# A graph network's first aggregation in 16-bit parts, with first products moved into it and a share of the score subtraction moved to ScalarE

## What is computed

```python
h = relu(layernorm(x))
x = x + gcn(h)      # h @ W0; out[d] = dinv[d] * (sum over edges of dinv[s]*hw[s] + dinv[d]*hw[d]) + b
h = relu(layernorm(x))
x = x + rgat2(elu(rgat1(h)))   # rgat1 with 4 heads, rgat2 with 1
# rgat: xr[r] = h @ W[r] for 3 relations; per edge alpha = leaky_relu(xr[r,dst]@q + xr[r,src]@k)
#       a = softmax of alpha over the edges of one dst;  out[dst] = sum of a * xr[r,src] + b
```

## Time and profile before

| | us |
|---|---|
| median of 3 runs | 1609.46 |
| lowest and highest run | 1606.19, 1611.54 |
| the profiled execution | 1607.11 |
| its span, first to last instruction | 1605.3 |
| PE busy | 1453.7 (91%) |
| DVE, ACT, POOL busy | 901.0, 274.0, 1000.9 |
| mean granted clock of PE | 0.932 of full speed |

### The profile page before, as it was taken

How to read it: one execution, slowest core, us unless ns; L and a number is a source line. 1 busy time by engine, 2 the same in 40 slices (tenths; PEclk the granted TensorE clock), 3 DMA queues, 4 the chain that set the end, 5 groups by cost and what they waited for, 6 DMA issues and landing times.

```text
span 1605.3 us, 24837 instructions
## 1 busy us (share of the span) xinstructions
PE 1453.7 (91%) x6446; PEld 878.0 (55%) x6450; DVE 901.0 (56%) x2002; ACT 274.0 (17%) x709; POOL 1000.9 (62%) x1112
## 2 busy tenths in 40 slices
PE   4988999999978999999699999769996999899996
PEld 2545555555566555666455555455553655455553
DVE  8677722334455888888688878406324445223333
ACT  2545300000011333323000124410110011000000
POOL 1599277666537777882477777336656662777673
PEclk9988999999987999899799999858997999899998
DMA  8300498899831131111588888701231111889898
GB/s 319 118 20 21 125 315 305 291 316 312 270 102 23 51 110 47 40 37 41 169 303 278 285 262 257 241 3 32 59 111 31 40 43 50 286 298 308 281 303 269
DMA packets 86811, 271.80 MB, mean 169 GB/s; under 512 B 32156, under 2 KB 32531, under 8 KB 86743
## 3 DMA queue, kind: packets, MB, share of 16 engines
q0 software_dynamic: 51072, 199.44, 39.3%
q1 hardware_dynamic: 34807, 65.62, 11.4%
q10 hardware_dynamic: 864, 5.90, 1.0%
HBM read 239.28 MB, written 31.62 MB: 169 GB/s over the span
## 4 chain that ended last, share of the span: by engine, by line
PE 61%; DMA 14%; POOL 10%; issue 7%; DVE 5%; ACT 1%; DVEq 1%; SPq 0%; POOLq 0%; ACTq 0%; PEldq 0%
PE ps L1293 12%; PE ps L1320 12%; PE ps L1359 12%; DMA ring<-keys,idxr 8%; POOL ring L519 8%; PE ps L1361 6%; PE ps L1362 6%; PE ps L1190 5%; DMA ring<-rows,idxr 3%; PE ps L1111 1%; PE ps L1236 1%; PE ps L1153 1%; PE ps L1254 1%; DVE zw L1020 1%; DVE hn L1017 1%
## 5 line engine op out<-in xcount | busy, mean ns | idle before, releaser
L1320 PE MATMUL ps<-wreg,hT 128*128 128x384 f32 x1440 | 486.7, 501 | 7.3 <-PEq L1313 6.6
L519 POOL DMA_INDIRECT ring<-keys,idxr x312 | 319.2, 1023 | 189.1 <-DMA ring<-keys,idxr 73.6
L488 POOL DMA_INDIRECT ring<-rows,idxr x304 | 303.7, 999 | 168.8 <-PEq L1348 60.9
L1320 PEld LDWEIGHTS ps<-wreg,hT 128*128 128x128 f32 x1440 | 280.6, 196 | 202.2 <-issue 23.5
L1359 PE MATMUL ps<-ring,zw 128*128 x664 | 224.0, 495 | 15.6 <-DVE zw L1088 15.0
L1293 PE MATMUL ps<-ring,zw 128*128 x664 | 221.3, 495 | 9.6 <-DVE zw L909 9.6
L488 POOL DMA_INDIRECT ring<-rows,idx x152 | 144.7, 952 | 97.1 <-PE ps L1293 66.0
L1359 PEld LDWEIGHTS ps<-ring,zw 128*128 128x128 f32 x664 | 124.7, 191 | 108.7 <-issue 34.2
L1086 DVE TENSOR_TENSOR ring<-ring,al x166 | 159.2, 959 | 39.4 <-SPq L406 30.7
L1293 PEld LDWEIGHTS ps<-ring,zw 128*128 128x128 f32 x664 | 127.5, 193 | 98.1 <-issue 15.3
L1091 DVE TENSOR_SCALAR zw<-iota_f,tl,al 128x128 f32<-128x128 f32 x166 | 60.8, 368 | 154.7 <-PE ps L1362 129.7
(11 more groups left out here) (189 smaller groups left out, 1314.0 us busy)
## 6 DMA issues: line engine op xcount, KB each, us to landing
wreg<-in_L_gnn_W SPq DMA_DIRECT2D x11, 2304.0 KB, 9.8
rows<-stage SPq DMA_DIRECT2D x30, 386.0 KB, 2.8
rows<-stage SPq DMA_DIRECT2D x30, 384.5 KB, 2.9
stT<-targets_row ACTq DMA_DIRECT2D x6, 960.0 KB
ring<-keys,idxr POOLq DMA_INDIRECT x312, 2.5
ring<-rows,idxr POOLq DMA_INDIRECT x304, 4.5
rows<-stT SPq DMA_DIRECT2D x10, 384.0 KB, 2.9
xs<-in_x SPq DMA_DIRECT2D x3, 1152.0 KB, 13.4
```

The source lines that it names most:

```text
L488: nc.gpsimd.indirect_dma_start(ring[:, t % (2 * RING), 0:WIDTH[l]], None, rows[l], bass.IndirectOffsetOnAxis(idx[:, t:t + 1], 0)).then_inc ...
L519: nc.gpsimd.indirect_dma_start(kb[:, n % KSEMS, t % KB, 0:4], None, keys[l], bass.IndirectOffsetOnAxis(idxr[:, t:t + 1], 0)).then_inc(k_in ...
L1320: last = mm(ps[:, 2 * (nt % 2) + h, 0:HALF], hT[:, k, nt * P:(nt + 1) * P], wreg[:, r % 2, k, h * HALF:(h + 1) * HALF], start=(k == 0), st ...
```

## The change

- **16-bit parts.** Each row of h @ W0, times `dinv`, is divided by a power of two of its own (`unit`; `put` is `dinv`/`unit`) and written as two 16-bit parts, upper and lower, side by side in the bytes of the 32-bit row. DVE finds largest and least value of a tile's rows (`peaks`) and makes the scales in three groups of tiles (`SPLITS`: 0 to 6, 7 and 8, 9) in `units`; ACT makes the upper parts, DVE the lower ones (`upper_parts`, `lower_parts`). The parts lie in hT (now laid out by node tile), and rows[0] has the scale as its extra column. The one-hots are 16-bit, scaled by the scale, in a ring of their own. Per edge tile PE runs four 16-bit matmuls (two halves, two parts) where it ran two of 32 bits. A node's own row comes in by four more matmuls that open the accumulator (`open_own`), no longer by DVE.
- **What moves.** The folds of the third relation go behind the pairs of node tiles 0, 1 and 2. The products with relation 0's weights of node tiles 0 to 7 (`EARLY = 8`) go behind `to_features` of the next tile, inside the first aggregation and its tail, with ACT's copy and the write to rows[1] from ACT's queue. They need 1/sqrt(variance) per tile, which DVE makes in `finish0` by an integer start value and four refinements (`inverse_root`, 14 dependent steps). `prepare(R - 1)` and the fill of `stage` go behind the one-hots of node tile 0.
- **Scores.** DVE subtracts for three heads only; ACT adds the fourth head's scores to the negated distance with two passes per pair. Both go to `scored2`, doubled. `MAX_AT` gets its own places for l = 1, `MASKS_AT` starts 16 halves later.

The diff, cut:

```diff
+EARLY = 8
+MASKS_AT = [(SURE_PAIRS - 3) * max(h + 1 - 2 * EARLY, 0) // (LAST_PAIRS_AT - 2 * EARLY) + 2 for h in range(LAST_PAIRS_AT)]
+SPLITS = ((0, 1, 2, 3, 4, 5, 6), (7, 8), (9,))
@@ ACT, behind the products with W0
                 keep_rows(nt, 0)
+                if nt == NT - 2:
+                    for t in SPLITS[0]:
+                        upper_parts(t)
+                if nt == NT - 1:
+                    for t in SPLITS[1]:
+                        upper_parts(t)
             keep_rows(NT - 1, 1)
+            for t in SPLITS[2]:
+                upper_parts(t)
@@ DVE, behind the sort
+            for t in SPLITS[0][5:]:
+                last = peaks(t)
+            units(0, last)
+            for t in SPLITS[0][:-1]:
+                lower_parts(t)
+            for t in SPLITS[1]:
+                last = peaks(t)
+            units(1, last)
+            for t in SPLITS[0][-1:] + SPLITS[1]:
+                lower_parts(t)
+            units(2, peaks(NT - 1))
+            lower_parts(NT - 1)
             prepare(1)
...
+            def begin0(j):
+                V.tensor_scalar(own[:, j % 2, :], ident[:, :], unit[:, j:j + 1], None, ALU.mult).then_inc(own_in, 1)
+                link(V.tensor_tensor(xs[:, j, :], xs[:, j, :], bias[:, :], ALU.add))
...
+            def inverse_root(j):
+                v, y, a = vare[:, j:j + 1], rstd[:, j:j + 1], pw[:, 0, 0:1]
+                link(V.tensor_scalar(v, mv[:, j, 1:2], EPS_LN, None, ALU.add))
+                link(V.tensor_scalar(y.bitcast(I32), v.bitcast(I32), -0.5, float(0x5f375a00), ALU.mult, ALU.add))
+                for n in range(4):
+                    link(V.scalar_tensor_tensor(a, y, v, y, ALU.mult, ALU.mult))
+                    link(V.tensor_scalar(a, a, -0.5, 1.5, ALU.mult, ALU.add))
+                    last = V.tensor_tensor(y, y, a, ALU.mult)
...
             for j in range(NT):
+                begin0(j)
                 with dve.Fori(bnd[j], bnd[j + 1]) as i:
+                    dve.wait_ge(g_in[0], 2 * i + (RING + 3))
                     for b in range(2):
-                        dve.wait_ge(w_used[0], t + (2 * RING - 1))
-                        V.tensor_scalar(zw[:, 0, b, 0, :], iota_f[:, 0:P], targets_at(i, b), row_at(i, b, D, D + 1), ALU.is_equal, ALU.mult).then_inc(w_in[0], 1)
+                        V.tensor_scalar(onehot_at(i, b), iota_h[:, 0:P], targets_at(i, b), row_at(i, b, D, D + 1), ALU.is_equal, ALU.mult).then_inc(w_in[0], 1)
+                if j == 0:
+                    prepare(R - 1)
+                    V.memset(stage[:, :, :], 1.0).then_inc(wq2_done, 1)
@@ PE
+            def early(nt):
+                pe.wait_ge(t_free, NW + NT + nt + 1)
+                for h in range(2):
+                    if nt >= 1:
+                        pe.wait_ge(early_in, 2 * (nt - 1) + h + 1)
+                    for k in range(KT):
+                        last = mm(ps[:, 6 + h, 0:HALF], hT[:, nt, k, :], wreg[:, 0, k, h * HALF:(h + 1) * HALF], start=(k == 0), stop=(k == KT - 1))
+                    last.then_inc(p_ready, 1)
             for j in range(NT + 1):
                 if j < NT:
-                    open_acc(0, j)
+                    open_own(j)
                     with pe.Fori(bnd[j], bnd[j + 1]) as i:
                         for b in range(2):
                             pe.wait_ge(w_in[0], 2 * i + (b + 1))
                             for a in range(2):
-                                last = mm(ps[:, 2 * (j % 2) + a, 0:HALF], zw[:, 0, b, 0, :], row_at(i, b, a * HALF, (a + 1) * HALF), start=False, stop=False, skip_group_check=True)
+                                for part in range(2):
+                                    last = mm(ps[:, 2 * (j % 2) + a, 0:HALF], onehot_at(i, b), parts_at(i, b, a, part), start=False, stop=False, skip_group_check=True)
                             last.then_inc(w_used[0], 1)
+                if j < 3:
+                    last_folds(NF + 2 * j, NF + 2 * j + 2)
                 if j >= 2:
                     for nt in ([j - 2] if j < NT else [j - 2, j - 1]):
                         to_features(1, nt)
+                        if 1 <= nt <= EARLY:
+                            early(nt - 1)
@@ ACT, per pair of edge tiles
+                act.wait_ge(nm_step[l], 2 * i + 2)
+                act.wait_ge(al_step[l], i + 1)
+                for b in range(2):
+                    last = nc.scalar.activation(scored2[:, side, b, 3, :] ..., negm[:, side, b, :] ..., ACT.Identity, bias=score_at(b), scale=-1.0)
+                last.then_inc(far_in, 1)
```

224 lines of the change are left out of this document (147 added, 77 removed).

## The result

| | before | changed |
|---|---|---|
| median of the runs, us | 1608.74 (4 runs) | 1665.2 (4 runs) |
| lowest and highest | 1606.19, 1611.54 | 1663.28, 1670.98 |
| the profiled execution | 1607.11 | 1670.98 |
| its span | 1605.3 | 1667.9 |
| mean granted clock | 0.932 | 0.907 |

The changed kernel is slower: ratio 1.035, 95% interval 1.0326 to 1.0373, or 56.5 us by the medians. The forecast was 1669, in a range of 1612 to 1702.

What follows compares the result with a forecast made beforehand. PE was taken to bind the first aggregation by only 0.04 us per tile over POOL, whose score batches DVE follows in the next stage. Terms 8.2 + 43.3 + 17.4 - 12 + 5 = +61.9 gave 1669 us, range 1612 to 1702.

Steps and rivals of the forecast that it cites:

- Part 1: Splitting rows into 16-bit parts ahead of the gathers: first gather at 207.9 us, +8.2 us (bounds +5 and +12).
- Part 2, the pauses: First aggregation: PE and DVE blocks at node-tile boundaries hold POOL's gathers for 79 us (bounds 66 and 92).
- The slack of 2.2 us: Eight-slot gather ring, 10.0 us against a 7.8 us slot cycle: PE pauses up to 2.2 us cost POOL nothing.
- Last matmul: End of the first aggregation: 501.0 us against 449.5, 7.8 us after the last gather at 493.2.
- The tail: From last aggregation matmul to keys: early products 6 and 7 stretch 10.2 us to 27.6, +17.4 (bounds +14 and +19).
- Part 3: Projections with scores and maxima: DVE lag, shorter DVE passes and quicker POOL gathers give -12 us (bounds 0 and -25).
- Rival C: Projection stage: the whole 64 us of PE come back, the rest as forecast, 1618 us; chance 0.08.
- The clock: PE's granted clock, plus weights and early rows moved beside the gathers: +5 us (bounds 0 and +25).
- rival B: PE's clock falls at each pause, early products 3 to 4 us dearer eight times: +28, 1697 us; chance 0.11.
- Rival D: Aggregation: two 16-bit matmuls cost as much as one of 32 bits, tile stays at 1.29 us: 1684 us; chance 0.04.
- Rival A: Aggregation: ring hides the blocks, each stage takes its busiest engine's need; faster, 1600 or 1570 us; chance 0.15.
- The sum: Whole kernel: 8.2 + 43.3 + 17.4 - 12 + 5 = +61.9 us on 1607.1, giving 1669.0.

Runs made afterwards that it cites:

- the run with six slots: Changed kernel with GpSimd allowed six row tiles in flight instead of eight in the first aggregation: 1689.78 us (one run).
- the run with one head: Changed kernel with VectorE's two passes of each pair cut to one head of four, other maxima left out: 1632.67 us (one run).
- the kernel before with ACT's scores and the other wait: Kernel before plus ScalarE's fourth-head scores, ScalarE waiting for the end of VectorE's first pass instead of an extra signal: 1606.22 us, ratio 0.9963.
- the quarters: Changed kernel with the six early-product blocks between tiles cut into four parts each, placed among the next tile's pairs: 1654.33 us, ratio 1.0287.

## Why the prediction was right, point by point

**Part 1** (+8.2, bounds 5 to 12): +11.2, inside the bounds. The scales of tiles 7 and 8, forecast for 195.6, came at 198.9 in this trace, when ACT, which had waited 3.74 us for them, begins their upper parts. The rest followed at the forecast distance: ACT's last copy ended at 201.0 instead of 197.6, the split at 207.0, and the first gather came 3.9 us behind. The 3 us are no more than what varies between traces of the same code: in the kernel with four early tiles ACT has the same wait (3.75 us), but the scales come at 193.2 and the first gather at 205.5. Over all traces the first gather starts 8.8 us later with the split than without it (209.7 against 200.9 on average).

**Part 2, the pauses** (79 us of held gathers, bounds 66 to 92): the gather of the last tile starts at 491.20; less 210.94 and 206.3 that is 74.0 us held. POOL's waits for PE sum to 92.4, of which 57 times about 0.3 would be there anyway, and 9 us stand behind that last gather, ahead of two gathers that only fill the ring. So 66 of the 74 us are waits for PE; the rest are gathers of 0.97 instead of 0.95 us and copies of indices between the last sixteen, which the forecast had left out. The pauses themselves: 11.5 to 12.7 us with queries (forecast 13.3), 9.1 to 10.2 without (forecast 10.6, as ACT's copy takes PE no time between). The slack of 2.2 us, worked out from the earlier trace rows, agrees with the run with six slots. The pair matmuls took 0.65 us a tile as assumed from the earlier trace rows: L1434 shows 326 ns for the record of a half with part, and 1.47 for a pair.

**Last matmul** (501.0): 504.8. The 7.8 us from last gather to last matmul were wrong here: an early block (487.6 to 499.4) lay between them, so it was 13.6. I had the block in the sum of pauses but not its meeting with the last tiles.

**The tail** (+17.4): 23.8 us against 10.2, +13.6, just under the lower bound of 14. The two products are there with 7.74 us each; ACT's copies and the last transposes overlapped more than I allowed. Together with the late last matmul the keys came at 528.62, forecast 528.6. That the two hit the same number is luck: +3.8 and -3.8.

**Part 3** (-12, bounds 0 to -25): -2. Inside the bounds, but 10 us off: this step failed, in two of its three terms.
- DVE's lag behind POOL's last batch (2.8 us) went as forecast: pair 66 begins 0.6 us behind its batch (783.03 against 782.42), so 2.2 came back.
- DVE's saving of 0.28 us a pair is 0.08. The pass is a quarter shorter (959 against 1225 ns), but the gap before it rose from 0.22 to 0.41, half of it by the extra signal. I had allowed 0.02 for that wait. Over 17 pairs that is 1.4 us, not 4.8.
- What POOL gets back (4 us) had the wrong sign: the twelfth batch is ready 253.5 us after the keys, before it was 250.4. The contention that the term rests on is real, as the run with one head shows: passes of a third and a quarter brought 24 us. The change cut DVE's time in both passes only from 2.45 in 2.70 us to 2.19 in 2.63. Yet that small cut is not worthless: in the kernel before with ACT's scores and the other wait, where the passes shrink by the same eighth, the batch comes 4.9 us sooner than before, about what I had. What took it away in the changed kernel comes with the extra signal. The Trainium skill ("SBUF — State Buffer", Who interferes with whom) describes a VectorE instruction with two SBUF inputs as holding up GpSimd's reads; the 1092 and 976 ns agree. That a small cut of such time buys a share in proportion was my own step. The pattern behind it has no explanation yet: in all nine kernels with the extra signal at full passes a key gather takes 1082 to 1105 ns, in the three without it 1057 to 1070. Whether DVE's signal or ACT's earlier passes do this wasn't tried.

The 64 us of PE, which the forecast gave no term of their own beside DVE's lag, were worth 4 to 6 us of stage: 324 to 326 us in the four kernels with eight early tiles and whole passes, 329.6 to 331.4 in the five with fewer and the same signal (the places of the maxima moved with them). Rival C, at 1618, is out: the stage of the kernel before was filled with PE, not bound by it.

**The clock** (+5): no term of its own, but there. It was 0.90 in the window of the aggregation against 0.98 before. Behind the long waits of the stream the granted clock stands at 0.50: the pair at 462.91 takes 2.74 us instead of 1.47, and the queries at 440.78 take 2.76 instead of 1.50. As an estimate, the records of tiles 4 to 9 that are longer in this way and stand in or right before a pause add up to 7 us; they are part of the pauses and the stretch measured above. So rival B's mechanism exists, but not its price: the early products, which it had 3 to 4 us dearer eight times, took 7.9 us each but for one of 8.45, and its 28 us appear nowhere. Rival D falls with the 0.65 us a tile. Rival A (the ring hides the blocks) falls with the cycle shown above and with the quarters.

**The sum** (+61.9, 1669.0): the profiled execution took 1670.98. Up to the keys the forecast was +68.9 and the trace has +68.9, by errors that cancel (Part 1 and the last matmul too early, the tail too long), and with the clock's few microseconds already in it. Behind them Part 3 gave 10 us less than forecast, the clock's 5 us did not come as a further term, and what lies behind the second aggregation's start, which I shifted whole, was 4.3 us shorter (813.0 against 817.3), inside the spread of the same instructions over the kernels: 61.9 + 10 - 5 - 4.3 = 62.6, the difference of the spans. So the total was right to 2 us for this execution, and to 4 for the median, while its terms were off by 3 to 10; that closeness is luck, the mechanism and the sign are not. Of the medians' 56.5 us, the trace puts all at or before the keys. The runs that undo parts put 51.3 us on the early products, 6.4 on the preparation and 10.6 on the folds, counted from the first gather; what is left is +11.2 of later gathers against -10.6 of faster matmuls.

## What to carry to other kernels

Before moving work into an engine's idle time, ask in what pieces the idle time comes. Here PE had two fifths of its time free, in gaps of 1 us, and a ring that could bridge 2 us. The 64 us of early products, in pauses of 9 to 13 us, cost 51 us; the same work in pieces of 2 us cost 13 less, and left where it was it cost 5. And where a stage is filled by one engine and waits on another, take work from the one that is waited for: 64 us off the filled engine gave 4 to 6, passes cut to a third and a quarter on the engine that the others wait for gave 40.

## What the runs showed of the hardware

- A POOL gather of keys took 0.95 us in the quiet (948 ns over 528 to 560 us), 1.09 beside DVE's full passes, 0.98 beside passes of a third and a quarter. That cut on DVE brought POOL's batches forward by 24 us in 253. The cut of an eighth in the change came with batches 3 us later, and the same cut without the extra signal with batches 5 us sooner.
- With half the pair matmuls left out, the granted clock went to 0.56 for most of 60 us, PE was busy 31.7 us of them, and a pair's four records took 1.46 us. With all eight it stayed at 0.94, PE was busy 36.2 us, and the eight took 1.47.
- One added signal ahead of a DVE instruction cost 0.09 us of DVE in a pair: the gap was 0.41 us with it in nine kernels, 0.32 to 0.33 in the two without it that have the same passes, 0.22 before.
